# A sort stage on VectorE as one maximum and one minimum over both row tiles, and the copies of idle keys ahead of the stage's compare

## What is computed

```python
# part 1: every position's correlations with all 4096 of its image, sorted, 256 ranks of them
x3 = _ln_c(x).reshape(B, M, F)                       # M = 4096, F = 256
corr = jnp.einsum('bmf,bnf->bmn', x3, x3) / F
s = -jnp.sort(-corr, axis=-1)                        # 16384 rows of 4096 keys
ranks = jnp.round(jnp.linspace(1.0, M - 1, 256)).astype(jnp.int32)
x = x + jnp.take(s, ranks, axis=-1).reshape(x.shape)
# part 2: a graph attention over 1048576 edges gives each token scores for 4 experts,
# the two best gate the experts' feed-forward results
alpha = segment_softmax(leaky_relu(a_src[src] + a_dst[dst]), dst)
scores = _layernorm(segment_sum(h[src] * alpha, dst)).reshape(M, HEADS, EXPERTS).mean(1)
out = sum_e gate_e * (gelu(t @ W1[e] + b1[e]) @ W2[e] + b2[e])
```

## Time and profile before

| | |
|---|---|
| time, median of 3 runs | 30711.82 us (30706.46 to 30725.64) |
| profiled execution, its span | 30706.0 us |
| sort of the 64 pairs on VectorE, first to last L1395 | 4701.4 to 27973.0 us |
| VectorE busy over the span | 27866.9 us |
| TensorE busy over the span | 26132.4 us |
| ScalarE busy over the span | 20334.5 us |
| GpSimd busy over the span | 19826.0 us |
| granted TensorE clock, mean | 0.922 |

### The profile page before, as it was taken

The page is one execution under the profiler, slowest core; times in us unless marked ns, Lnnn a source line. Parts: engine busy times, 40 slices in busy tenths (PEclk is TensorE's granted clock), DMA queues, the critical chain, the costliest instruction groups (busy, mean ns, idle before and its releaser), DMA issues. The chain is left out here.

```text
span 30706.0 us, 514061 instructions
## 1 busy us (share of the span) xinstructions
PE 26132.4 (85%) x182003; PEld 12435.8 (40%) x182004; DVE 27866.9 (91%) x31378; ACT 20334.5 (66%) x30319; POOL 19826.0 (65%) x9076
## 2 busy tenths in 40 slices
PE   3888889989999999999999999989999999982473
PEld 2555543333333333333333333333333333332473
DVE  6888858999999999999999999999999999996435
ACT  1777777767767767767776776767777777763720
POOL 0000007898888888888888888888888898402610
PEclk8999999999999999999999999999999999996655
DMA  2000000000000000000000000000000000000104
GB/s 93 2 2 2 2 19 4 7 7 7 7 7 7 12 7 7 7 7 7 7 12 7 7 7 7 7 6 7 13 7 7 7 6 7 7 5 13 15 11 136
DMA packets 651242, 393.57 MB, mean 13 GB/s; under 512 B 425132, under 2 KB 604336, under 8 KB 646448
## 3 DMA queue, kind: packets, MB, share of 16 engines
q1 hardware_dynamic: 338034, 311.42, 3.2%
q0 software_dynamic: 290304, 22.40, 1.1%
q10 hardware_dynamic: 20288, 25.70, 0.2%
HBM read 196.49 MB, written 162.34 MB: 12 GB/s over the span
## 5 line engine op out<-in xcount | busy, mean ns | idle before, releaser
L1584 POOL DMA_INDIRECT sorted_d<-word_s,place_s x8192 | 18974.3, 2316 | 2642.8 <-issue 2476.8
L1496 ACT ACTIVATE z<-psum 128x1024 f32<-128x1024 f32 x10089 | 10181.7, 1054 | 2004.0 <-PE psum L1223 1258.5
L1395 DVE TENSOR_TENSOR arena<-arena 128x1024 f32<-128x1024 f32 (+16 forms) x5760 | 10843.3, 1883 | 442.8 <-ACT arena L1492 397.0
L1396 DVE TENSOR_TENSOR arena<-arena 128x1024 f32<-128x1024 f32 (+16 forms) x5760 | 10837.1, 1881 | 0.0
L1223 PE MATMUL psum<-z,net 64*64 64x512 f32 x72504 | 9163.8, 601 | 140.3 <-ACT z L1496 111.2
L1496 ACT ACTIVATE cst<-psum 128x1024 f32<-128x1024 f32 x5015 | 5303.4, 1058 | 979.2 <-PE psum L1223 635.0
L1223 PE MATMUL psum<-cst,net 64*64 64x512 f32 x36040 | 4826.4, 602 | 77.9 <-ACT cst L1496 51.0
L1223 PEld LDWEIGHTS psum<-z,net 64*64 64x64 f32 x72504 | 2425.6, 131 | 5275.3 <-issue 5178.5
L1216 PE MATMUL psum<-rows,arena 128*128 128x256 f32 x8192 | 2017.6, 402 | 1629.4 <-ACT arena L1492 1597.1
L1578 POOL DMA_DIRECT2D word_s<-words_d x64 | 37.5, 586 | 4830.5 <-ACT cst L1496 4702.1
L1038 ACT ACTIVATE arena<-cst,arena 128x128 bf16<-128x128 f32 x8320 | 2632.8, 389 | 610.1 <-PE psum L966 513.4
(11 more groups left out here) (231 smaller groups left out, 23519.1 us busy)
## 6 DMA issues: line engine op xcount, KB each, us to landing
sorted_d<-word_s,place_s POOLq DMA_INDIRECT x8192
y_d<-ys SPq DMA_DIRECT2D x256, 256.0 KB
arena<-y_d SPq DMA_DIRECT2D x64, 1024.0 KB, 5.5
arena<-in_x SPq DMA_DIRECT2D x34, 512.0 KB, 5.1
x<-in_x SPq DMA_DIRECT2D x65, 256.0 KB
xnt_d<-arena SPq DMA_DIRECT2D x32, 512.0 KB, 3.1
hk_d<-arena SPq DMA_DIRECT2D x32, 512.0 KB, 4.3
arena<-hk_d SPq DMA_DIRECT2D x4, 4096.0 KB
```

What stands on the lines that cost most here:

```text
L1395: nc.vector.tensor_tensor(hi_out, hi_in, lo_in, ALU.max)
L1396: return nc.vector.tensor_tensor(lo_out, hi_in, lo_in, ALU.min)
L1496: last = nc.scalar.activation(flat, bank, ACT.Abs)
L1584: pool.indirect_dma_start(out=b.sorted_d[:, :], out_offset=bass.IndirectOffsetOnAxis(ap=place_s[:, s, j:j + 1], axis=0), in_=word_s[:, s, ...
```

## The change

A stage is one maximum and one minimum over both halves, and counts `sorted_` up once instead of twice. All waits on `sorted_` are counted by stages. The exception is `FIRST_MERGE`, whose two parts lie in different buffers: two compares, one count. `bring_together` still runs once for each row tile, with one count. Every stage from 1 on waits for the whole stage before it. The copies of idle keys are issued ahead of the stage's compare, behind its waits.

```diff
@@ sparse
                 if s == N_FULL:
-                    dve.wait_ge(sorted_, (i + 1) * 2 * N_FULL)
+                    dve.wait_ge(sorted_, (i + 1) * N_FULL)
                     dve.wait_ge(carried, (i + 1) * N_CARRIED)
@@ carry
-                dve.wait_ge(sorted_, (i * N_FULL + (s + 1)) * 2)
+                dve.wait_ge(sorted_, i * N_FULL + (s + 1))
                 nc.vector.tensor_copy(edges_of(target[:, 0:to], p, which),
                                       edges_of(source[:, 0:to], p, which)).then_inc(carried, 1)
@@ sort
                     whole = edge if s < FIRST_MERGE else 2 * M
-                    for h in range(2):
-                        here = slice(h * whole // 2, (h + 1) * whole // 2)
-                        if s == 0 and h == 0:
-                            wires_done(dve, body, in_body)
-                            if after_first:
-
-                                dve.wait_ge(tailed, i * SPARSE)
-                        elif s > 0:
-
-                            across = (p, k) in ((1024, 1024), (1024, 512)) or s == FIRST_MERGE
-                            dve.wait_ge(sorted_, (i * N_FULL + s) * 2 + (0 if across else h - 1))
-                            if h == 0 and k in (p // 4, p // 16):
-                                dve.wait_ge(carried, i * N_CARRIED + carried_before(s))
-                        if s == 0:
-                            last = compare(fresh[:, here], target[:, here], p, k)
-                        elif s == FIRST_MERGE:
-                            old, new = slice(here.start, min(edge, here.stop)), slice(max(edge, here.start), here.stop)
-                            if old.start < old.stop:
-                                last = compare(source[:, old], target[:, old], p, k)
-                            if new.start < new.stop:
-                                last = compare(fresh[:, new], target[:, new], p, k)
-                        elif (p, k) == (1024, 1024):
-                            last = bring_together(source, target, h)
-                        else:
-                            last = compare(source[:, here], target[:, here], p, k)
-                        last.then_inc(sorted_, 1)
-                        for which in range(2):
-                            if h == 0 and k == p >> (which + 1):
-                                f = first_of(p)
-                                carry(keys[f % 2], keys[(f + 1) % 2], whole, p, which, i, f)
+                    if s == 0:
+                        wires_done(dve, body, in_body)
+                        if after_first:
+
+                            dve.wait_ge(tailed, i * SPARSE)
+                    else:
+
+                        dve.wait_ge(sorted_, i * N_FULL + s)
+                        if k in (p // 4, p // 16):
+                            dve.wait_ge(carried, i * N_CARRIED + carried_before(s))
+                    for which in range(2):
+                        if k == p >> (which + 1):
+                            f = first_of(p)
+                            carry(keys[f % 2], keys[(f + 1) % 2], whole, p, which, i, f)
+                    if s == 0:
+                        last = compare(fresh[:, 0:edge], target[:, 0:edge], p, k)
+                    elif s == FIRST_MERGE:
+                        compare(source[:, 0:edge], target[:, 0:edge], p, k)
+                        last = compare(fresh[:, edge:whole], target[:, edge:whole], p, k)
+                    elif (p, k) == (1024, 1024):
+                        bring_together(source, target, 0)
+                        last = bring_together(source, target, 1)
+                    else:
+                        last = compare(source[:, 0:whole], target[:, 0:whole], p, k)
+                    last.then_inc(sorted_, 1)
@@ scalar, front
-                        act.wait_ge(sorted_, ((pair - 1) * N_FULL + read) * 2)
+                        act.wait_ge(sorted_, (pair - 1) * N_FULL + read)
```

## The result

The changed kernel takes 32421.19 us (median of 4, 32418.33 to 32481.39), the kernel before 30710.28 us (median of 4 by then). The ratio is 1.056, 95% interval 1.0547 to 1.0573: 1711 us slower. The forecast was 30784 us with 30675 to 30860 as its range, so the time lies far outside.

What follows compares the result with a forecast made beforehand. VectorE's chain was taken as the bound: drains against removed instructions -0.30, added waits +1.64, `normalise` -0.21, together +1.13 us a pair, x 64 = +72 us on 30712, so 30784 us, range 30675 to 30860.

Steps and rivals of the forecast that it cites:

- The bound before, and the drain on VectorE: Each pair lasts as long as VectorE's chain; waiting for the instruction just ahead costs it 0.115 us.
- The instructions removed: In the sort's stages 88 fewer maxima and minima a pair, each saving its fixed 0.067 us: 5.90 us a pair.
- The waits added: 40 new drained stages a pair at 0.14 us (0.115 drain, 0.025 behind it), 5.60, plus second waits, 1.64.
- k = p/16: Sort stages whose second wait's sequencer step now sits behind the drain: 5 x 0.09 = 0.45 us a pair.
- k = p/4: Sort stages where the copy, now first, brings a third wait: 5 x 0.19 = 0.95 us a pair.
- k = p/2: Sort stages whose copy waits for the stage's own value: 4 x 0 to 0.12, middle 0.24 us a pair.
- -0.30 + 1.64 a pair: VectorE's sort chain: drains less removed instructions give -0.30 us, waits that are more than one add 1.64.
- The first rival: In VectorE's sort all 88 fixed parts are saved and no wait costs: 30395 us, faster; chance 8%.
- the second: In the ten stages with second waits the sequencer steps overlap the drain: 30699 us, not slower; chance 21%.
- the third: In the 25 plain sort stages the wait value's register step also costs 0.09 us: 30928 us; chance 11%.
- `normalise`: Its wait for ScalarE's root absorbs what stages 1 to 8 gain or lose: 0.21 us a pair taken back.
- one clause of the first paragraph: GpSimd's scatter ends before the sort and still does after a change of a microsecond or so a pair.

Runs made afterwards that it cites:

- e3: The kernel before with every stage's two halves waiting for the whole stage ahead, instructions as short as before: 31076.15 us, ratio 1.0111.
- e4: The kernel before with `normalise` one stage later (NORM_AT 9 instead of 8): 30605.04 us, ratio 0.9959.
- e5: The changed kernel with each stage's minimum replaced by a one-input reduction of the same length, keys not sorted: 30804.72 us, ratio 1.0027.
- e6: The changed kernel with the copies of idle keys issued behind the compare again, stages still fused: 32397.91 us, ratio 1.0545.
- run 6906: Not a run's label: 6906 is the number of scatters begun before the sort's end in the changed kernel's own run, 32421.19 us.
- e9: The kernel before with two more stages, (512, 512) and (2048, 2048), waiting for the whole stage ahead: 30745.57 us, ratio 1.0008.
- e10: The changed kernel with each stage's minimum replaced by a copy of the lower keys, keys not sorted: 38789.54 us, a single execution.

## Why the prediction was wrong

**The bound before, and the drain on VectorE: right.** VectorE's chain set the pair's length, ScalarE still waits 1438.4 us for it in the stretch of the earlier trace rows, and the sort gained or lost what its chain did.

**The instructions removed: right.** 88 a pair, and only the fixed part. The 0.067 holds at 4096 columns too (pitch 4.34, 15378.45 to 15382.79).

**The waits added: right in kind, a little too dear.** The drain is +0.12 at a plain entry. Of the 0.025 behind it, priced from two drained starts, 0.007 is there in the median of the run (here 3.81 from 15400.39 to 15404.20, where 3.80 is plain). 40 times 0.123 instead of 0.14 is 0.7 us a pair less. k = p/16 came as 0.20 (0.115 + 0.09), k = p/4 as 0.28 where 0.115 + 0.19 was set, k = p/2 as 0.18 where 0.115 + 0.06 was set: there is a step for the second wait of the same value. The sort from its first to its last L1395 takes 31 us more, the forecast had 72. Of the 31, 16 are the wait of the next paragraph, so the chain itself costs 15 us where -0.30 + 1.64 a pair made 86. The first rival (the drain hides), the second (the added steps are not seen) and the third (every stage exposes one) are all refuted by these rows. In e3 prices read from the changed kernel's trace gave 358 us, and 354 were measured.

**`normalise`: right that the wait is a real loss, wrong in what it takes back.** e4 shows the first. The forecast had the wait swallow what stages 1 to 8 lose, 0.21 us a pair or 13 us. It grew by 16 instead, from 105.1 to 121.2:

```profile
DVE rs L1589 <- ACT std L1496: 99.3, 43, 4.2
...
DVE rs L1589 <- issue: 21.9, 10, 2.3
```

In e3 it is 95.0 us, in e5 175.5 and in e6 180.9. What moves it was not found, and no run was made for it.

**What failed** is one clause of the first paragraph: "GpSimd's scatter ends before the sort does", which "keeps that in either direction for a change of a microsecond or so" a pair. It took GpSimd's pace for its own, put the scatter's delay at nothing without a row for it, and asked only whether the sort's end would move. Between its long holds GpSimd's pace was VectorE's: one scatter a two-input instruction. The edit nearly leaves VectorE's time alone and doubles the length of its instructions in 44 of 46 stages, and that is what GpSimd goes by. It was to be read from the trace of the kernel before. A scatter took 1.90 us beside instructions of 2.20 and 1.63 beside instructions of 1.94, with 0.30 between two, so its pitch was VectorE's pitch; no rival in the list was about GpSimd.

An estimate from that trace would have been: one scatter for each of the 92 maxima and minima, and the 16.8 a pair that began elsewhere before (1004 in the 59.9 pairs that the scatter spanned), if no scatter is held long. That gives 6960 in 64 pairs and 1232 behind the sort, 1577 us at 1.28 each. In the run 6906 were begun and 1286 were left. They took the 1738 us from the last L1395 to the last scatter: 1646 us at 1.28 each, and some 90 more, the pauses for the next words above all. That the long holds would go was not to be known before e3.

An engine that waits for another's instructions to end can become the bound though the bound engine's own time stays the same.

## What to carry to other kernels

GpSimd's indirect DMAs beside VectorE instructions with two SBUF inputs, or two inputs followed by a fast copy, are paced by VectorE's instruction boundaries, so fusing VectorE work slows GpSimd even where VectorE itself gets no slower. Before lengthening VectorE's instructions, compare the pitch of GpSimd's instructions with VectorE's and work out the lateness of the slower engine from the new pitch. In an undrained VectorE chain one semaphore wait on the instruction just ahead costs VectorE 0.12 us and can end a long hold of GpSimd: in e9 two such waits a pair cost 25 us of the time and brought the scatter's end 3.2 ms forward.

## What the runs showed of the hardware that was not expected

- One issued scatter was shut out for 146 us by VectorE instructions, to the next drained start; with a drain in each stage none was held for 20 us. Why some scatters slip in at an undrained start and others do not is open.
- It is the indirect DMA that is held. GpSimd's plain DMAs that load the words took 0.58 us in the median in the changed kernel too, at most 0.73. Of the 128 loads of words and places there, 77 began and ended within one L1395 or L1396.
- A one-input reduction of 4.28 us let three scatters through, a copy of 2.15 to 2.22 us none.
- In e10 all engines slowed while the scatter ran: TensorE is busy 28.8% at a mean granted clock of 0.61, between its levels of 1.2 GHz (0.5) and 2.4 GHz (1.0), and 99% at 1.00 when it is over. Columns: stretch, its length, busy us of TensorE, its weight loads, VectorE, ScalarE and GpSimd, clock, DMA share, GB/s.

```profile
9000.00:13000.00 4000.00, 1152.78 (x6398) 440.44 (x6399) 816.40 (x458) 738.28 (x802) 2994.28 (x2522) 0.61 0.02 3
...
19000.00:23000.00 4000.00, 3964.45 (x27116) 1664.06 (x27112) 3359.39 (x2025) 3060.00 (x3387) 0.00 (x0) 1.00 0.02 8
```

In the first of these stretches TensorE's weight loads waited 2689.2 us for nothing that the trace shows, in single waits of up to 44.7 us; and VectorE stood for up to 1010.5 us at a time, in which 718 scatters followed each other, at 1.28 us or a little more. A long row of scatters at their full pace went together with engines that hardly ran. In e5, where some three followed each other at that pace beside each long reduction, TensorE was busy 3686 to 3701 us of each 4000, as in the kernel before. It seems that such a row keeps the other engines back, but this is one execution, and no run shows what holds them or which comes first.
